# Edge rows gathered four steps ahead, sixteen experts written out, and VectorE's low halves in quarters

## The reference

```
h   = layernorm(x)                                    # 1250 x 512
msg = relu(h[src] + edge_attr @ W_e + b_e)            # 21250 edges, sorted by dst
agg = segment_sum(msg, dst)
h   = (1 + eps) * h + agg
h   = silu(bn(silu(bn(h @ W1 + b1)) @ W2 + b2))       # 512 -> 1024 -> 512
x   = x + h
a   = softmax(layernorm(x) @ gate)                    # 16 experts
for each expert e: the 156 tokens of highest a
    y = gelu(layernorm(x)[tokens] @ w1[e] + b1[e]) @ w2[e] + b2[e]
    x[tokens] += a * y
```

## Time and profile before

| | |
|---|---|
| median of 3 runs | 761.31 us (760.77 to 762.72) |
| the profiled execution | 758.0 us |
| its span in the profile | 756.2 us |
| granted PE clock, mean | 0.888 of full speed |
| edge loop, by the gathers' first and last start | 52.6 to 329.7 us |
| busy over the span: PE, DVE, ACT, POOL | 70%, 63%, 47%, 48% |

### The profile page before, as it was taken

How to read it: one execution, slowest core, us unless ns; L and a number is a source line. 1 busy time by engine, 2 the same in 40 slices (tenths; PEclk the granted TensorE clock), 3 DMA queues, 4 the chain that set the end, 5 groups by cost and what they waited for, 6 DMA issues and landing times.

```text
span 756.2 us, 15773 instructions
## 1 busy us (share of the span) xinstructions
PE 530.1 (70%) x5273; PEld 382.1 (51%) x5273; DVE 478.9 (63%) x1042; ACT 357.5 (47%) x610; POOL 360.1 (48%) x284
## 2 busy tenths in 40 slices
PE   1527868788787777769988995712577866968791
PEld 1314445454454444445544554511577866958781
DVE  4944657586666666666539657777566665857650
ACT  0603545355444445454437406530267656756661
POOL 1717777777777777740000000130266456545552
PEclk9999989899989999999998997755589878889996
DMA  7376787868777686643300004150358678688632
GB/s 182 120 215 190 196 197 183 203 180 200 197 182 201 175 203 175 172 115 113 112 0 1 1 0 136 56 182 11 90 148 259 170 212 225 173 218 212 200 52 34
DMA packets 79647, 111.34 MB, mean 147 GB/s; under 512 B 32207, under 2 KB 40842, under 8 KB 79615
## 3 DMA queue, kind: packets, MB, share of 16 engines
q0 software_dynamic: 43712, 53.95, 29.6%
q1 hardware_dynamic: 34637, 56.16, 25.2%
q10 hardware_dynamic: 1266, 0.81, 0.5%
HBM read 95.35 MB, written 15.35 MB: 146 GB/s over the span
## 4 chain that ended last, share of the span: by engine, by line
PE 28%; DMA 19%; issue 17%; POOL 16%; DVE 11%; ACT 5%; POOLq 1%; SPq 0%; ACTq 0%; DVEq 0%
PE bank L1202 16%; POOL big L413 11%; DMA big<-node_rows,src_now 9%; DMA big<-token_rows,idx 6%; POOL out L435 3%; PE bank L1218 2%; POOL big L426 2%; PE bank L1182 2%; DVE stats L699 2%; DMA pair<-in_src 1%; DMA out<-rows_z,idx 1%; PE bank L1345 1%; DVE rows_z L710 1%; PE bank L1184 1%; ACT pair L579 1%
## 5 line engine op out<-in xcount | busy, mean ns | idle before, releaser
L413 POOL DMA_INDIRECT big<-node_rows,src_now x170 | 211.2, 1242 | 63.6 <-issue 43.8
L1202 PE MATMUL bank<-big,pair 128*128 128x156 f16 (+2 forms) x1824 | 177.3, 261 | 7.2 <-DVE big L912 5.3
L1202 PEld LDWEIGHTS bank<-big,pair 128*128 128x128 f16 x1824 | 147.9, 104 | 32.9 <-issue 6.7
L541 ACT ACTIVATE big<-bank 125x512 f16<-125x512 f32 x136 | 81.2, 597 | 127.1 <-PE bank L1184 126.6
L845 DVE SCALAR_TENSOR_TENSOR big<-bank,big 125x512 f16<-125x512 f32 x136 | 90.3, 686 | 41.8 <-ACT big L541 39.0
L1182 PE MATMUL bank<-big,ident_scaled 125*125 125x512 f16 x136 | 59.3, 436 | 71.4 <-DMA big<-node_rows,src_now 70.6
L435 POOL DMA_INDIRECT out<-rows_z,idx x32 | 60.0, 1874 | 61.1 <-ACT rows_z L673 38.2
L426 POOL DMA_INDIRECT big<-token_rows,idx x32 | 55.6, 1738 | 68.3 <-DVE idx L1056 51.9
L454 POOL TENSOR_TENSOR big<-aggT,big 125x512 f16<-125x512 f32 x10 | 11.3, 1155 | 159.3 <-ACT big L602 159.3
L1158 PEld LDWEIGHTS bank<-onehot,big 125*128 125x128 f16 x1400 | 62.5, 101 | 31.9 <-issue 7.5
L1182 PEld LDWEIGHTS bank<-big,ident_scaled 125*125 125x125 f16 x136 | 19.0, 140 | 117.3 <-DMA big<-node_rows,src_now 113.6
(11 more groups left out here) (197 smaller groups left out, 864.5 us busy)
## 6 DMA issues: line engine op xcount, KB each, us to landing
raw<-in_L_ffn_w SPq DMA_DIRECT2D x32, 1024.0 KB, 6.4
edge<-in_edge_attr SPq DMA_DIRECT2D x35, 140.0 KB
node_rows<-big SPq DMA_DIRECT2D x10, 448.0 KB
raw<-in_L_gnn_W SPq DMA_DIRECT2D x16, 256.0 KB, 7.2
big<-node_rows,src_now POOLq DMA_INDIRECT x170, 5.9
xs<-in_x SPq DMA_DIRECT2D x5, 448.0 KB
out<-xs SPq DMA_DIRECT2D x5, 448.0 KB
token_rows<-big SPq DMA_DIRECT2D x5, 448.0 KB
```

The costliest lines, as they stand in the source:

```text
L413: pool.indirect_dma_start(to, None, table, bass.IndirectOffsetOnAxis(src_now[place][:, b, j:j + 1], 0)).then_inc(row_in[b * J + j], 16)
L541: act.activation(msg[:, b * J + j, 0, :], rows32[b] if j == Z else bank[j][0:P, :], ACT.Relu).then_inc(msg_hi, 1)
L1202: last = pe.matmul(bk, weights(i, k), values(j, k), start=(begin and p == k == 0), stop=(end and p == 2 and k == n - 1), skip_group_check= ...
```

## The change

The edge loop's rows get four steps of buffers instead of two: steps 0 and 1 of a group in `big`, steps 2 and 3 in the two `pair16` tiles, which are free in this stage. POOL's loop over the 34 steps is written out: it waits once for a step, then issues five gathers, and takes the indices straight from `src_i`. A step's rows have three semaphores (rows 0 and 1, row Z, rows 3 and 4), so PE waits for both rows of a pair. `edge_transposes` moves from row 3 to row 1, and ACT's copy of its result from row 4 to row 3.

The experts are written out on all engines, so the hardware loops go. The gathered tokens have four buffers (XR), the weighed outputs three (YR), the indices and gates one for each expert. The raw weights have five buffers (RH): the two of before, and three in tiles whose content is dead by then (`edge_home`, `xs_home`, `aggT`), and SP loads six experts' weights before the stage begins. POOL issues `gather(e+3)` ahead of `scatter_end(e-2)` and `scatter(e-1)`. DVE's and ACT's orders are changed as well, and `expert_low` is four instructions of 512 columns in place of one of 2048.

```diff
-    CREDIT = 3 * JP
+    RING = 4
+    CREDIT = RING * JP
+    XR = 4
+    YR = 3
+    RH = 5
...
+        def rows_landed(w, g, r, place, n):
+
+            return w * (16 * n * (SB // RING + (r < SB % RING))) + (g * (8 * n) + n * (16 - 8 * (place % 2)))
...
+        late_rows = [pair16[i][0:P].rearrange("p w a (s h) -> p (w a s) h", h=H)
+                     .rearrange("p (s w) h -> p s w h", w=2) for i in range(2)]
+
+        def row(r, j):
+
+            return rows[:, r * J + j, :, :] if r < 2 else late_rows[r - 2][:, j, :, :]
+
+        def row32(r):
+            return row(r, Z).rearrange("p w h -> p (w h)").bitcast(F32)
...
-        rows32 = [big[0:P, (b * J + Z) * H:(b * J + Z + 1) * H] for b in range(2)]
...
+            def load_expert(e, m):
+                w = (fw1_t, fw2_t)[m]
+                sp.dma_start(e_raw[e % RH][:, m, :].rearrange("p (k f) -> p k f", k=HK), w[e]
+                             ).then_inc(ew_in[e % RH][m], 16)
+
+            def reload(e):
+                for m in range(2):
+                    sp.wait_ge(e_lo, (e - RH) * 2 + m + 1)
+                    load_expert(e, m)
...
+            sp.wait_ge(W1_lo, HK)
+            for m in range(2):
+                load_expert(0, m)
+            sp.wait_ge(agg_ready, 1)
+            for m in range(2):
+                load_expert(2, m)
+            sp.wait_ge(W2_lo, F1)
+            for m in range(2):
+                load_expert(1, m)
+            reload(5)
...
+            for t in range(0, 4, XG):
+                store_tokens(t, XG)
+            sp.wait_ge(x2_out, 16 * NT)
+            sp.wait_ge(xn2_ready, NT)
+            for m in range(2):
+                load_expert(3, m)
+            for t in range(4, NT, XG):
+                store_tokens(t, XG)
+            sp.wait_ge(xt2_ps, NT)
+            for m in range(2):
+                load_expert(4, m)
+            for e in range(6, EX):
+                reload(e)
...
-            def step(w, g, b, place):
-                n = w * SB + (g * 2 + b)
-                if b == 0:
-
-                    pool.wait_ge(msg_ps, n * JP + JP)
-                    pool.wait_ge(rowsz_used, n + 1)
+            with pool.Fori(0, n_pass) as w:
+                for i in range(SB):
+                    ago = RING if i >= SB % RING else SB % RING
+                    pool.wait_ge(msg_ps, w * (SB * JP) + (CREDIT + (i - ago + 1) * JP))
+                    pool.wait_ge(rowsz_used, w * SB + (RING + i - ago + 1))
                     pool.sem_inc(pool_turn, 1)
-                    pool.tensor_copy(src_now[place][:], src_i[:, bass.ds(g * 2, 2), :]).then_inc(src_ready, 1)
-                    pool.wait_ge(src_ready, w * (SB // 2) + g + 1)
-                for j in range(J):
-                    if j == Z:
-                        pool.wait_ge(rowsz_used, n + 2)
-                    else:
-                        pool.wait_ge(msg_ps, n * JP + JP + rank(j) + 1)
-                    pool.sem_inc(pool_turn, 1)
-                    to, table = (rows32[b], node_rows32) if j == Z else (
-                        rows[:, b * J + j, :, :].rearrange("p w h -> p (w h)"), node_rows)
-                    pool.indirect_dma_start(to, None, table,
-                                            bass.IndirectOffsetOnAxis(src_now[place][:, b, j:j + 1], 0)
-                                            ).then_inc(row_in[b * J + j], 16)
-
-            run_steps(pool, n_pass, SB, step)
+                    for j in range(J):
+                        pool.indirect_dma_start(row32(i % RING) if j == Z else
+                                                row(i % RING, j).rearrange("p w h -> p (w h)"), None,
+                                                node_rows32 if j == Z else node_rows,
+                                                bass.IndirectOffsetOnAxis(src_i[:, i, j:j + 1], 0)
+                                                ).then_inc(row_in[i % RING][trio(j)], 16)
...
+            for e in range(XR - 1):
+                gather(e)
+            for e in range(EX):
+                if e + XR - 1 < EX:
+                    gather(e + XR - 1)
+                if e >= 2:
+                    scatter_end(e - 2)
+                if e >= 1:
+                    scatter(e - 1)
...
-            def expert_low(e, b, m):
-                dve.wait_ge(e_hi, num(e) * 2 + m + 1)
-                dve.scalar_tensor_tensor(out=pair16[b][:, 1, m, :], in0=raw[b][:, m, :], scalar=W_SCALE,
-                                         in1=pair16[b][:, 0, m, :], op0=ALU.mult, op1=ALU.subtract).then_inc(e_lo, 1)
+            def expert_low(e, m):
+                dve.wait_ge(e_hi, e * 2 + m + 1)
+                for c in range(HK):
+                    cols = slice(c * H, (c + 1) * H)
+                    last = dve.scalar_tensor_tensor(out=pair16[e % 2][:, 1, m, cols], in0=e_raw[e % RH][:, m, cols],
+                                                    scalar=W_SCALE, in1=pair16[e % 2][:, 0, m, cols],
+                                                    op0=ALU.mult, op1=ALU.subtract)
+                last.then_inc(e_lo, 1)
...
-            def expert(e, first=False, ahead=3):
-                if ahead >= 1:
-                    expert_low(after(e, 1), 1 - e[1] % 2, 0)
-                if not first:
-                    weigh(after(e, -1))
-                low_h(e)
-                if ahead >= 1:
-                    columns(after(e, 1))
-                if ahead >= 2:
-                    indices(after(e, 2))
-                if ahead >= 1:
-                    expert_low(after(e, 1), 1 - e[1] % 2, 1)
-                if ahead >= 3:
-                    choose(after(e, 3))
+            def expert(e):
+                if e + 1 < EX:
+                    expert_low(e + 1, 0)
+                if e + 3 < EX:
+                    indices(e + 3)
+                low_h(e, 0)
+                if e >= 1:
+                    weigh(e - 1)
+                if e + 1 < EX:
+                    expert_low(e + 1, 1)
+                low_h(e, 1)
+                if e + 1 < EX:
+                    columns(e + 1)
+                if e + 4 < EX:
+                    choose(e + 4)
...
-                        pe.wait_ge(row_in[b * J + j], i * 16 + 16)
-                        pe.matmul(bank[j][0:P, :], ident_scaled[0:P, 0:P], rows[:, b * J + j, 0, :],
+                        pe.wait_ge(row_in[r][trio(j)], rows_landed(w, g, r, place, 2))
...
-                    if j == 3:
+                    if j == 1:
...
-            def expert(e, first=False, ahead=3):
+            def expert(e):
                 up(e, 0)
-                if not first:
-                    turn_back(after(e, -1))
+                if e + 3 < EX:
+                    pick_tokens(e + 3)
+                if e >= 1:
+                    turn_back(e - 1)
                 up(e, 1)
-                if ahead >= 2:
-                    pick_tokens(after(e, 2))
-                if ahead >= 1:
-                    turn_rows(after(e, 1))
+                if e + 1 < EX:
+                    turn_rows(e + 1)
                 down(e)
```

409 lines of the change are left out of this document (191 added, 218 removed).

## The result

The changed kernel took 732.84 us in the median of four runs (727.37 to 740.44), the kernel before 761.22: a ratio of 0.960, 95% interval 0.954 to 0.966. It is faster, by 28 us where I forecast 54, and 727.37 to 740.44 lies beyond my range (694 to 727).

The account below looks back on a forecast made before the run. POOL's issue rate was taken to bound the edge loop, the scatter-gather-landing ring the experts. 756.2 - 16.0 - 38.2 = 702.0 us span, 703.8 for the execution, 707.1 for the median; own range 694 to 716, with rivals 694 to 727.

Parts of the forecast that it names:

- 16.0 us gained: Edge loop: removing 17 index copies gains 17.0 us, less 1 us at the end where row 3 waits for row 4.
- the second rival: Edge loop stays at 8.2 us a step through longer landings or the engines' ring: 723 us, 12 in 100.
- the slack: Edge loop: 7.7 - 6.2 us in each step was to hide PE's waiting for two rows at a time.
- I take 10.0 us: Experts: a turn set by the chain across PE, ACT and DVE, bounds 9.2 to 11.4, in place of 12.46 us.
- 2.71 us: Experts: DVE's four quarters of 678 ns each, in place of 2.28 us, counted in the turn's chain.
- The DMA rival: Experts: DMA engines not filled beyond 0.9 make turns 11.4 us while weights load, 14 us more, 721; 16 in 100.
- 6.0 us for an expert unhindered and 9.2 in the dense window: Experts: POOL's time per expert fits under the 10.0 us turn, so the quarters get nothing but their DVE cost.
- 148.7: Experts: fourteen turns at 10.0 us and a last at 8.74, in place of 186.9 us, so 38.2 us gained.
- The tail behind the sixteenth `turn_back`: After the experts' last turn: same steps as before, left unchanged in the sum.
- the 694: Lower end of the forecast's range, given for experts' turns of 9.2 us.
- the 716: Upper end of the forecast's own range, before it was widened to 727 for the rivals.
- Third rival: Experts: DVE waits for POOL's four DMA instructions, 4.8 us more a turn, 67 us, 775; 5 in 100.

Follow-up runs that it names:

- r1_after: The changed kernel itself, unedited, run once more on another chip beside the kernel before: 723.0 us, ratio 0.949.
- e3_before_quarters: The kernel before with only `expert_low` cut into four operations of 512 columns: 752.7 us, ratio 0.991.
- t1_split: Changed kernel, each four-operation low half cut in two by operations reading PSUM, gelu's second low half behind all: 748.4 us, ratio 0.971.
- e2_row3: Changed kernel with the edge transposes back in row 3 and ACT's copy of them in the last row: 740.7 us, ratio 0.967.
- s3_chain: Changed kernel with gelu's second low half between the second matrix's second and third low-half operations, column copy behind them: 697.4 us, ratio 0.917.
- e7_spread: Changed kernel with each matrix's low half in two trains of two operations, other DVE work between them: 705.2 us, ratio 0.926.

## Why the prediction was wrong

Three terms of the sum failed: the edge loop's gain, POOL's time in the experts, and the tail.

**Edge loop.** The step "16.0 us gained" was right where updates are in time: r1_after gains 17.4 us at W1, POOL issues each 1.54 us, and the moved transposes cost nothing (PE waits for landings only). In the profiled run of the result the second rival held, "the PE, ACT, DVE ring can't hold 7.7", at 12 in 100 and with 16 us. Its cause was none that I had weighed, PE's late updates. The kernel before bears them without loss (e3_before_quarters: 0.7 us in the mean, and W1 at 335.4): POOL's pace of 8.15 us a step (277.1 us for 34) is near the 8.35 that late updates allow, and the new pace of 7.7 is well below it. Cost: 12.8 us of 16. I had read the slack (7.7 against a step of 6.1) from a trace in which the handovers were 0.12 us.

**Turns.** "I take 10.0 us" was a mis-sized term on the safe side: 9.41 undisturbed. Half of the difference is the quarters, which I had added up as 2.71 us; they overlap, and the next operation starts 2.41 us behind the first one's start (580.47, 582.88). The DMA rival did not come: from 559 to 597 us the DMA engines were busy for 0.95 of the time, with turns of 9.41.

**POOL.** The step that failed is that POOL needs "6.0 us for an expert unhindered and 9.2 in the dense window (8.01 + 1.2), under 10.0 either way. So I give the quarters nothing but their cost". Those 9.2 us came from an expert that stood between two with idle time. With every turn dense, 18 to 20 of some 57 DMA instructions of POOL take over 3 us in the changed kernel's three traces, up to 4.85 in this one; in the stretch from 585.13 to 598.65 two scatters and two gathers fill 13.5 us with 12.1 of work. POOL falls behind by two to three experts, and turns of 12 to 17 us follow: fifteen turns took 160.9 us, where 9.41 each would be 141.2. Cost against the forecast: 160.9 for 148.7, 12.2 us.

**Tail.** "The tail behind the sixteenth `turn_back` have the same steps as before, and I leave them" failed by 12.8 us: with POOL late two more experts' scatters, 7.0 us each, stand ahead of the last.

12.8 + 12.2 + 12.8 = 37.8 us; 1.2 us came back ahead of the first `turn_back`, and 702.0 + 37.8 - 1.2 is the span of 738.6. The median stands 7.6 us under that execution, before it stood 3.3 above. Of the range, the 694 is 0.9 us lower than its terms give (707.1 less 14 x 0.8 and 1.0), and the 716 has no term; neither bears on what failed.

**Third rival.** DVE did not wait for POOL: the quarters take 673 to 694 ns in all 128 cases. The first of the four rows of that line's view (ns min/median/max):

```profile
L979 DVE SCALAR_TENSOR_TENSOR pair<-raw,pair x56: 673/680/693, 431.9 to 698.5; 128x512 f16<-128x512 f32 x56
```

The opposite side decided: POOL waits for DVE. The Trainium skill, "SBUF — State Buffer", section "Who interferes with whom", says that the instruction which comes second blocks fully until the first has ended. For DVE's side no run here agrees. For POOL's, the extra 2.67 us (4.13 less 1.46) agree with a block over the whole train of 2.48, not over one operation. By the same section an operation with at most one SBUF input, outside the modes that take both ports, doesn't contend, so t1_split's weighing should have opened a gap; its 0.58 us let nothing through, be it that it was too short or no gap.

**Open.** What makes PE's updates late on three of five chips and in the first run, while POOL issues, was not found. The transposes' place is excluded (e2_row3); the number of PE's updates and POOL's own were not tried on such a chip. Nor is it known when POOL gets through. That it needs its own length without two-input operations fits t1_split, but the scatter at 632.72 in s3_chain passed at a bare end of an operation; and that it needs such an end doesn't fit e7_spread, where several ended the set time behind an operation that its successor overlaps (the gather at 551.93, 0.88 us behind 554.13). Untested, too, is gelu's second low half wholly ahead of the second matrix, as in the kernel before, with the rest of the change: it would shorten the chain without a cut.

## What to carry over

A change that takes away one engine's slack has to be priced with every instruction of that engine at its length beside full neighbours, not at the length in one dense stretch between idle ones; and an engine that runs late through a loop hands its backlog to the tail. When a large operation is cut, put the operation that the next engine waits for into the cut: that was worth 25 us here (723.0 to 697.4 on one chip), and the cut alone nothing that could be told from noise in this kernel. And run the unchanged kernel beside the experiments on each chip before believing that an edit cured something or that it had nothing to do with it.

## What was not expected of the hardware

The chips differ in one thing that, of these kernels, only the changed one and its variants feel. Beside POOL's gathers, one each 1.5 us, PE's semaphore updates reached ACT 0.9 to 2.2 us behind the row in the mean on three chips and 0.12 us on two others, with the same kernel (W1 at 334.2 against 319.2 us), while the kernel before took 760 to 762 us on four of the five, with either. In the late traces the updates come at two places of a gather, about 0.6 and 1.4 us behind its start, and the delay ends with POOL's last gather. And POOL's scatter, 1.46 us alone, took up to 6.26 us beside a DVE that never paused.
